# Attention, LayerNorm and a routed block on one core: the second normalisation's variance reused for the dense rows, and the softmax maximum subtracted as the bias of one exponential per head

## What is computed

```python
x = _layernorm(x + attn(x))
x = _layernorm(x + ffn(x))
```

```python
def _layernorm(x, axis=-1, eps=1e-05):
    m = jnp.mean(x, axis=axis, keepdims=True)
    v = jnp.var(x, axis=axis, keepdims=True)
    return (x - m) / jnp.sqrt(v + eps)
# picked tokens, 16 heads, 127 x 127 scores each
a = jax.nn.softmax(sc + m_sel[:, None], axis=-1)
```

## Time and profile before

| | us |
|---|---|
| three runs, median (lowest to highest) | 6889.99 (6887.44 to 6895.84) |
| the profiled execution | 6889.63 |
| its span in the profile | 6887.9 |
| `routed_block`, from about 6100 to the end | 788 |

### The profile page before, as it was taken

The page is one execution under the profiler, slowest core; times in us unless marked ns, Lnnn a source line. Parts: engine busy times, 40 slices in busy tenths (PEclk is TensorE's granted clock), DMA queues, the critical chain, the costliest instruction groups (busy, mean ns, idle before and its releaser), DMA issues. The chain is left out here.

```text
span 6887.9 us, 128540 instructions
## 1 busy us (share of the span) xinstructions
PE 6057.8 (88%) x48057; PEld 4345.6 (63%) x48057; DVE 5879.6 (85%) x4549; ACT 5853.6 (85%) x5874; POOL 147.9 (2%) x217
## 2 busy tenths in 40 slices
PE   7499999999999999999999999999999999935555
PEld 4366666666666666666666666666666666625444
DVE  5299889988999889988998899889988888858886
ACT  1199999999999999999999999999999999911222
POOL 0000000000000000000000000000000000011000
PEclk8799999999999999999999999999999999966677
DMA  7422112221222112211221122112211111122220
GB/s 267 161 69 80 56 48 66 78 63 47 63 76 69 48 55 79 72 46 50 82 77 47 47 80 78 47 49 74 79 54 47 46 45 48 37 72 54 55 58 21
DMA packets 469580, 463.10 MB, mean 67 GB/s; under 512 B 163636, under 2 KB 351956, under 8 KB 467864
## 3 DMA queue, kind: packets, MB, share of 16 engines
q1 hardware_dynamic: 463512, 448.56, 21.5%
q0 software_dynamic: 5376, 5.30, 0.3%
HBM read 291.45 MB, written 162.14 MB: 66 GB/s over the span
## 5 line engine op out<-in xcount | busy, mean ns | idle before, releaser
L659 ACT ACTIVATE a_wave<-a_ps_turn 128x1024 f32<-128x1024 f32 x5120 | 4903.7, 1356 | 66.0 <-PE a_ps_turn L593 65.7
L593 PE MATMUL a_ps_turn<-a_q_r,a_k_r 64*128 64x512 f32 x20480 | 3384.8, 397 | 358.7 <-ACT a_wave L659 280.2
L676 DVE SCALAR_TENSOR_TENSOR a_weight<-a_wave,a_head_c,a_weight 128x2048 f32<-128x2048 f32 x1536 | 3613.2, 2352 | 81.3 <-DVE a_weight L676 0.5
L593 PE MATMUL a_ps_turn<-a_q_r,a_rounder 64*128 64x512 f32 x20480 | 3237.2, 391 | 4.3 <-issue 4.3
L593 PEld LDWEIGHTS a_ps_turn<-a_q_r,a_k_r 64*128 64x128 f32 x20480 | 1951.7, 184 | 1510.6 <-ACT a_wave L659 828.8
L593 PEld LDWEIGHTS a_ps_turn<-a_q_r,a_rounder 64*128 64x128 f32 x20480 | 1978.5, 185 | 240.6 <-issue 8.9
L676 DVE SCALAR_TENSOR_TENSOR a_weight<-a_wave,a_head_c 128x2048 f32<-128x2048 f32 x512 | 1203.5, 2351 | 559.5 <-ACT a_wave L659 559.5
L653 ACT ACTIVATE a_weight<-a_weight,a_head_c 128x2048 f32<-128x2048 f32 x512 | 1178.5, 2302 | 36.6 <-issue 31.4
L613 PE MATMUL a_ps_out<-a_weight,a_v_r 128*32 128x512 f32 x4096 | 546.4, 605 | 8.4 <-ACT a_weight L653 6.8
L613 PEld LDWEIGHTS a_ps_out<-a_weight,a_v_r 128*32 128x32 f32 x4096 | 80.6, 108 | 195.1 <-issue 184.4
L572 POOL COPY a_head_c<-a_table 128x5 f32 (+1 forms) x128 | 56.8, 444 | 5619.2 <-ACT a_weight L653 5619.2
(11 more groups left out here) (234 smaller groups left out, 2093.9 us busy)
## 6 DMA issues: line engine op xcount, KB each, us to landing
a_q_r<-qs_d SPq DMA_DIRECT2D x256, 320.0 KB
qs_d<-a_q_hl SPq DMA_DIRECT2D x224, 320.0 KB, 5.3
a_k_r<-k_d SPq DMA_DIRECT2D x512, 128.0 KB
a_q_r<-qs_d SPq DMA_DIRECT2D x256, 160.0 KB
k_d<-p_k_hl SPq DMA_DIRECT2D x8, 4096.0 KB, 12.8
a_k_r<-k_d SPq DMA_DIRECT2D x512, 64.0 KB
o_d<-a_out SPq DMA_DIRECT2D x512, 34.0 KB
num<-o_d SPq DMA_DIRECT2D x32, 512.0 KB
```

The source lines that it names most:

```text
L593: last = nc.tensor.matmul(ps_turn[slot_of(r, s, f)][:, half, :], exact(w(rows[half])), exact(q_r[rows[half], k, f, :]), start=(i == 0), st ...
L659: nc.scalar.activation(wave[:, s // 2 % 2, f, s % 2, :], ps_turn[slot_of(r, s, f)][:].rearrange("p a b -> p (a b)"), ACT.Sin, scale=TURN_I ...
L676: return v.scalar_tensor_tensor(both(weight[:, i, :, :]), both(wave[:, i % 2, f, :, :]), head_c[:, k, f:f + 1], to, ALU.mult, ALU.add)
```

## The change

The dense rows: `x1` is the result of a LayerNorm without affine part, so its mean is taken as zero and its variance is worked out from the variance v of the normalisation that made it, as v / (v + eps): `moments[:, 1, :, 1]` times the square of the reciprocal deviation `spread[:, 1, :]`. The scaling then needs no mean. The softmax: instead of subtracting the maximum from all scores, the maximum is negated (`below`) and given as the bias of the exponential. As a bias is one number per partition, the exponential is issued head by head, sixteen times, and the last one signals `exped`.

```diff
--- before.py
+++ after.py
@@ -769,6 +769,7 @@
         qk_pad = sb("qk_pad", [P, 2 * H, 32])
         qk_t = sb("qk_t", [P, 2 * QH, P])
         logits, probs_t = sb("logits", [P, H, P]), sb("probs_t", [P, H, P])
+        below = sb("below", [P, H])
         peak, total, inv_total = sb("peak", [P, H]), sb("total", [P, H]), sb("inv_total", [P, H])
         att, att_t = sb("att", [P, D]), sb("att_t", [P, KC, P])
         xa, h2, h2_t, g_t = sb("xa", [P, D]), sb("h2", [P, D]), sb("h2_t", [P, KC, P]), sb("g_t", [P, FB, P])
@@ -1071,7 +1072,9 @@
                         run(spread[:, 1, :], spread[:, 1, :], ACT.Sqrt, "dev2")
                     if back is not None:
                         ready("shifted")
-                        run(logits[:, :, 0:KSEL], logits[:, :, 0:KSEL], ACT.Exp, "exped")
+                        for n in range(H):
+                            ins = nc.scalar.activation(logits[:, n, 0:KSEL], logits[:, n, 0:KSEL], ACT.Exp, bias=below[:, n:n + 1])
+                        ins.then_inc(S["exped"], 1)
                         ready("p_turned")
                         run(probs_t[0:KSEL, 8:16, :].rearrange("p a b -> p (a b)"), flat(Bk[0:KSEL, 2:4, :]), ACT.Copy, "p_hi")
                     if front is not None:
@@ -1186,7 +1189,10 @@
                     if front is not None:
                         draw_o(1)
                     if back is not None:
-                        moments_of(step, x1, 2, "dense_var", EPS_LN / 4)
+                        v.memset(spread[:, 2, :], 0.0)
+                        step(v.tensor_tensor(moments[:, 2, :, 0], moments[:, 1, :, 1], spread[:, 1, :], ALU.mult))
+                        step(v.tensor_tensor(moments[:, 2, :, 1], moments[:, 2, :, 0], spread[:, 1, :], ALU.mult))
+                        v.tensor_scalar(spread[:, 2, :], moments[:, 2, :, 1], EPS_LN / 4, None, ALU.add).then_inc(S["dense_var"], 1)
                     if front is not None:
                         add_bias(0)
                     if back is not None:
@@ -1200,8 +1206,7 @@
                         step(v.reciprocal(spread[:, 2, :], spread[:, 2, :]))
                         dve.wait_ge(S["dense_stored"], 16 * back + 16)
                         for t in range(LT):
-                            ins = v.tensor_scalar(dense[:, t, :], x1[:, t, :], moments[:, 2, t, 0:1], spread[:, 2, t:t + 1],
-                                                  ALU.subtract, ALU.mult)
+                            ins = v.tensor_scalar(dense[:, t, :], x1[:, t, :], spread[:, 2, t:t + 1], None, ALU.mult)
                         ins.then_inc(S["dense_ready"], 1)
                     if front is not None:
                         add_bias(1)
@@ -1240,8 +1245,7 @@
                                                          ALU.mult, ALU.add)
                         step(ins)
                         step(v.tensor_reduce(peak[:], logits[:, :, 0:KSEL], AX.X, ALU.max))
-                        v.tensor_tensor(logits[:, :, 0:KSEL], logits[:, :, 0:KSEL], peak[:].unsqueeze(2).broadcast_to([P, H, KSEL]),
-                                        ALU.subtract).then_inc(S["shifted"], 1)
+                        v.tensor_scalar(below[:], peak[:], -1.0, None, ALU.mult).then_inc(S["shifted"], 1)
                     if front is not None:
                         ready_f("dev2")
                         step_f(v.reciprocal(spread[:, 1, :], spread[:, 1, :]))
```

## The result

| | before | changed |
|---|---|---|
| median of six runs (lowest to highest), us | 6890.82 (6884.09 to 6896.45) | 6846.42 (6843.18 to 6852.34) |
| span of the profiled execution, us | 6887.9 | 6844.3 |

The ratio is 0.9936 with an interval of 0.9926 to 0.9945: 44.4 us faster. The forecast was 6858.7, a gain of 30.9, with a range down to 6848.

The account below looks back on a forecast made before the run. It took VectorE's chain of waits in routed_block's seven repeated bodies as the bound: 14.3 + 3.2 + 14.2 - 0.75 = 30.9 us off 6889.6, giving 6858.7 us, range 6848 to 6872.

Parts of the forecast that it names:

- the three parts: In routed_block: moments of x1 save 14.3 us, scaling 3.2, softmax maximum 14.2 over seven bodies.
- 4.75 us of exponentials: ScalarE softmax: sixteen exponentials starting 0.29 us apart take 4.75 us, replacing one of 1.90 us.
- waiting at the copy: DVE's copy L1267 behind the softmax: 0.08 us of waiting for TensorE's transposes of the exponentials.
- TensorE's clock: Rival: closed pause before L1003 brings the clock back sooner; up to 1.3 us a body, 9 us, 6850; 10%.
- part 3: Softmax maximum (L1243, L1045): negated maximum as bias saves 2.03 us in each of seven bodies, 14.2 us.
- The last back half: Eighth back half, running alone at the end: exponentials finish 0.75 us later; parts 1 and 2 give nothing.
- Part 1: Moments of x1 (L1126 to L1132): bias add L1149 starts about 2.38 us earlier in six bodies, 14.3 us.
- No overlap among the exponentials: Rival at the softmax: sixteen exponentials take 6.35 us, gain falls to 19 us, 6870.7; 12%.
- Slower by a low clock at L940: Rival at the projections: L940 falls to 1.2 GHz, 7.07 us become 14.1, total 6901; 3%.
- bias adds waiting over 1 us: Sign of being wrong at bias add L1149: waiting over 1 us, where about 0.6 us was forecast.
- TensorE's clock moved from its levels: Sign of being wrong: PE's clock rows in the profile moved from their levels.

Follow-up runs that it names:

- the three kernels with part 3: Part 3 alone added to the kernel before, 6868.75 us; the full change, 6846.42 us; the full change with the moments edit undone, 6858.08 us.
- the filled pause: Kernel before, plus twelve idle transposes on TensorE between the exponentials' transposes and L1003: 6886.97 us, ratio 0.9996.
- with the stall moved: Changed kernel with the moments edit undone and GpSimd's addition to x_in also waiting for DVE's angles: 6844.34 us, ratio 0.9933.
- part 1 alone: Kernel before with only the x1 variance worked out from the second normalisation's; scaling and softmax as before: 6880.85 us, ratio 0.9985.
- the pause opened again: Changed kernel, exponentials signalled after eight and after sixteen, so transposes start sooner and a pause returns ahead of L1004: 6854.20 us, ratio 0.9950.
- two pauses filled: Changed kernel plus idle transposes, 30 after the product with v and 28 after the output projection: 6834.85 and 6835.03 us, ratios 0.9919.
- a third pause: Changed kernel with those 30 and 28 idle transposes and 20 more behind the threshold, ahead of the turn of hn: 6833.19 us, ratio 0.9915.

## Why the prediction was wrong

The terms of the three parts were right where they stand: 2.40 for 2.38, 0.49 for 0.45, 2.12 for 2.11 us on DVE, 4.77 for 4.75 us of exponentials, 0.09 for 0.08 us of waiting at the copy.

**The step that failed** is TensorE's clock, which the sum has at nothing: it takes every TensorE piece behind the softmax at the length it had before. Measured, the stretches of VectorE that wait for such pieces are 10.2 us shorter in the six gaps. I had this as a rival with its cause, "the change shortens PE's pause between L997 and L1003 from 2.96 us to nothing", but gave it 10%, "up to 1.3 us a body" and 9 us in all, which set the lower end of the range. Measured, it is 1.0 us at the ranking in the later bodies and 1.36 in the earlier, 0.2 to 0.6 ahead of `xm` and 0.1 to 0.3 ahead of `o_t` in five of the six gaps, together 1.7 to 1.9 us there and 0.95 in the first of the six. I priced the two groups that the pause joins and not those behind them, L1023 and L934, for which DVE also waits. My argument against it, that L1003 to L1009 is dense today and still at 0.50, rested on the second body, of which I had written that the others repeat it. For TensorE they don't: in the later ones L1009 takes 4.05 us instead of 6.85, and the granted clock is 1.00 from 6601.2 to 6603.6. There the clock does rise behind L1003, and in the changed kernel, where 3.8 us of transposes stand right ahead, it rises inside L1003. The Trainium skill (TensorE: Matmul & The Clock Gate, What's actually happening) has the clock follow how busy PE has been recently; the three kernels with part 3 agree (L1003 at 2.2 to 3.0 us), as does the filled pause (2.05).

**The last back half** I had 0.75 us longer; from the last `w_diag` to the end it is 2.25 us shorter. The exponentials do take longer there, but the body ahead of it gained 1.6 us by the clock too, and the product with v took 5.33 us instead of 7.01. In the other kernels it takes 4.48 to 7.01 us there, so a fixed term was the wrong kind, and that it came out at 5.33 here is no merit of the change that the runs show.

**Part 1's 14.3 us** hold in the changed kernel by size, not by the reason given. I took the statistics as what puts DVE behind the projection. Of the 10.65 us from the angles to the bias add 4.4 were GpSimd's addition holding DVE, which the prediction doesn't name; of POOL it says only that its work "is timed from the end of a body, which no edit reorders". The saving hung on that stall. Undone, part 1 costs 11.7 us, not 14.3; alone it gives 10.3; with the stall moved the six gaps are as short without it as with it.

**The rivals.** No overlap among the exponentials is out, 4.77 us against 6.35. Slower by a low clock at L940 did not happen in the changed kernel, L941 takes 7.07 us in all bodies; with part 1 alone its milder form did. Of my signs of being wrong, two came: bias adds waiting over 1 us, in three bodies (1.6 to 1.7 us), where the stall had moved and no time was lost, and TensorE's clock moved from its levels, which was the miss.

**What stays open** is which course of work brings the full clock to which piece. That part 3 brings the gain is shown; that it is by the closed pause fits the pause filled before and the pause opened again, but both moved the clock elsewhere too, and part 3 also starts the transposes later, which no run takes apart. Five kernels with filled or opened pauses moved it, and one of them, with two pauses filled, did what I expected at the MLP and in the total, though not at the bias add; the traces show where it rose and fell, and no rule by which I could have said so beforehand. The gaps settle to one value (92.16 and 92.15 us before, 85.33 twice in the changed kernel) or to two in turn (89.5 and 91.4 with part 1 alone, 82.6 and 84.6 with two pauses filled). So each kernel falls into a course of its own; what sets it no run here isolates.

## What to carry to other kernels

When an edit changes the pauses of TensorE, price every later TensorE group for which the bounding engine waits at both clock levels, not only the groups that border the pause, and let the range hold both. Before crediting a saving of instructions to an engine, look for one tiny instruction of several microseconds in the same stretch: it is another engine's hold, and moving that by one semaphore may give the same time. Idle transposes are a trial, not a rule: ahead of two groups on the chain they gave 11.5 us, ahead of two others on the chain (L1003 in the kernel before, L935 as a third pause) nothing clear, and ahead of the transposes of the exponentials, for which DVE hardly waits, they cost 10.5.

## What the runs showed of the hardware

A GpSimd addition of 128x2048 in SBUF (4.51 us) made VectorE instructions of 0.17 us (`tensor_scalar`, `scalar_tensor_tensor` and `tensor_tensor` of 128x8) last up to 4.5 us, while `scalar_tensor_tensor` with one operand in PSUM and `bn_stats` ran beside it undisturbed. A one-pointer, one-operation `tensor_scalar` on 256 fp32 columns follows its like every 0.264 us, with two pointers and two operations every 0.324. Sixteen exponentials of 127 columns with a pointer as bias start 0.29 us apart.
